# Attention kernel: the zeros in the unused corner of the weights go, and the row-sum matmul is split in two instead

## The reference

```python
scores = jnp.einsum('bhid,bhjd->bhij', Q, K) / jnp.sqrt(jnp.float32(hd))
delta = t[:, None] - t[None, :]
decay = jnp.where(delta < 0, 0.0, -delta.astype(jnp.float32) ** ALPHA)   # ALPHA = 1
scores = jnp.where(delta < 0, -jnp.inf, scores) + decay
attn = jax.nn.softmax(scores, axis=-1)
out = jnp.einsum('bhij,bhjd->bhid', attn, V)
```

## Time and profile before

| what | value |
|---|---|
| median of 3 runs | 1163.5 us (1161.0 to 1164.31) |
| the profiled execution's own time | 1161.0 us |
| its span, first to last instruction | 1159.4 us |
| around the span | 1.6 us |
| mean granted TensorE clock | 0.973 |
| PE busy | 1078.0 us, 93% of the span |
| DVE busy | 932.2 us, 80% |
| ACT busy | 796.4 us, 69% |
| POOL busy | 527.1 us, 45% |

### The profile page before, as it was taken

The page is one execution under the profiler, slowest core; times in us unless marked ns, Lnnn a source line. Parts: engine busy times, 40 slices in busy tenths (PEclk is TensorE's granted clock), DMA queues, the critical chain, the costliest instruction groups (busy, mean ns, idle before and its releaser), DMA issues.

```text
span 1159.4 us, 44674 instructions
## 1 busy us (share of the span) xinstructions
PE 1078.0 (93%) x18369; PEld 723.4 (62%) x18400; DVE 932.2 (80%) x2102; ACT 796.4 (69%) x1685; POOL 527.1 (45%) x969
## 2 busy tenths in 40 slices
PE   5899999999999999999999999999999999998551
PEld 3567666667666666676666666666666766664320
DVE  5858998888888888888988888888888888887563
ACT  5566777787766777777677777766777777666432
POOL 1133445454554544554545455545454555445331
PEclk9999999999999999999999999999999999999765
DMA  9666666766556667556676675655667656563231
GB/s 277 136 144 140 129 153 149 160 144 144 138 119 154 152 148 165 130 139 144 128 158 153 148 166 130 146 135 127 156 155 150 157 138 144 132 114 102 65 69 43
DMA packets 204833, 161.80 MB, mean 140 GB/s; under 512 B 150449, under 2 KB 150705, under 8 KB 204529
## 3 DMA queue, kind: packets, MB, share of 16 engines
q1 hardware_dynamic: 199888, 141.86, 55.6%
q0 software_dynamic: 4736, 17.04, 3.8%
HBM read 40.87 MB, written 16.78 MB: 50 GB/s over the span
## 4 chain that ended last, share of the span: by engine, by line
PE 80%; DVE 10%; issue 3%; SPq 3%; DMA 2%; ACT 2%; POOL 0%; DVEq 0%; POOLq 0%; ACTq 0%
PE f_job L1404 51%; PE f_st L1505 6%; PE f_o L1524 6%; PE f_o L1527 4%; PE f_job L1580 4%; PE f_job L1480 3%; PE f_job L1562 2%; SPq L357 2%; PE f_job L1570 1%; PE f_job L1488 1%; DMA f_x2Tl<-f_x2l 1%; DMA f_stacks<-f_mrow 1%; DVE f_rmax L1044 1%; DVE f_x L1117 1%; DVE f_x2l L1138 1%
## 5 line engine op out<-in xcount | busy, mean ns | idle before, releaser
L538 POOL TENSOR_SCALAR_AFFINE_SELECT f_PT<-f_PT 64x512 f32<-64x512 f32 (+1 forms) x256 | 181.9, 729 | 120.3 <-ACT f_PT L705 81.7
L1404 PE MATMUL f_job<-f_xTh,f_wqh 128*128 128x256 f16 x512 | 140.8, 275 | 15.2 <-DVE f_wkl L903 14.4
L1404 PE MATMUL f_job<-f_xTl,f_wqh 128*128 128x256 f16 x512 | 140.2, 274 | 0.0
L1404 PE MATMUL f_job<-f_xTh,f_wql 128*128 128x256 f16 x512 | 140.2, 274 | 0.0
L1404 PE MATMUL f_job<-f_xTh,f_wkh 128*128 128x256 f16 x512 | 140.0, 273 | 0.0
L1404 PE MATMUL f_job<-f_xTh,f_wkl 128*128 128x256 f16 x512 | 140.0, 273 | 0.0
L1404 PE MATMUL f_job<-f_xTl,f_wkh 128*128 128x256 f16 x512 | 139.9, 273 | 0.0
L675 ACT ACTIVATE f_stage<-f_job,f_bias 128x256 f16<-128x256 f32 x256 | 106.2, 466 | 34.1 <-PE f_job L1404 29.6
L1030 DVE SCALAR_TENSOR_TENSOR f_stage<-f_job,f_bias,f_stage 128x256 f16<-128x256 f32 x256 | 110.5, 477 | 20.5 <-ACT f_stage L675 18.4
L551 POOL TENSOR_TENSOR f_z<-f_z,f_x 128x512 f32<-128x512 f32 x62 | 78.1, 1280 | 101.7 <-ACT f_z L757 101.7
L705 ACT ACTIVATE f_PT<-f_st 128x512 f32<-128x512 f32 x192 | 113.0, 602 | 14.0 <-PE f_st L1505 14.0
(11 more groups left out here) (201 smaller groups left out, 3052.6 us busy)
## 6 DMA issues: line engine op xcount, KB each, us to landing
f_stacks<-f_stage SPq DMA_DIRECT2D x380, 128.0 KB
f_xin<-x SPq DMA_DIRECT2D x32, 512.0 KB, 4.1
f_x<-x SPq DMA_DIRECT2D x32, 512.0 KB, 4.4
out<-f_z POOLq DMA_DIRECT2D x31, 512.0 KB, 5.4
f_Vmix<-f_V SPq DMA_DIRECT2D x32, 256.0 KB, 3.3
f_Vmix<-f_V SPq DMA_DIRECT2D x64, 128.0 KB, 3.3
f_stacks<-rows_const SPq DMA_DIRECT2D x3, 512.0 KB, 4.7
f_stacks<-wqT SPq DMA_DIRECT2D x2, 512.0 KB, 5.1
```

The costliest lines, as they stand in the source:

```text
L538: nc.gpsimd.affine_select(out=d, in_=d, compare_op=ALU.is_ge, fill=0.0, base=odd * SUB, pattern=[[0, 4], [0, TP], [1, SUB]], channel_multi ...
L1404: mm = pe.matmul(dst, lhs[a](c), rhs[b](c), start=(n == 0), stop=(n == 3 * KC - 1))
```

## The change

DVE no longer zeroes the corner: clear_past, its 16 calls and its semaphore go, and with them weigh's wait. In exchange the row sums of an opening step no longer read the corner. There, the matmul of 256 columns for each of the four heads becomes two: one over the lower 64 partitions for the 64 columns of chunk 0, and one over 128 partitions for the other 192 columns. The four heads' matmuls of 64 columns come first, then the four of 192. In the other 24 steps of 32 the instructions of weigh are as before.

```diff
-            def clear_past(s, g):
-
-                until(dve, pv_done, 4 * s + g - 1)
-                nc.vector.memset(PT[g % 2][SUB:P, :, 0:SUB], 0.0).then_inc(past_cleared, 1)
-
...
             front_stats(2)
-            clear_past(0, 0)
-            clear_past(0, 1)
             for s in range(STEPS - 1):
...
                 if has(k):
                     normalise(k, 3)
-                if s and s % PER == 0:
-                    clear_past(s, 1)
                 if has(k - 1):
                     find_scale(k - 1, 0)
...
                 normalise(s, 2)
-                if n % PER == 0:
-                    clear_past(n, 0)
                 split_max(n)
...
                     pe.wait_ge(v_mixed, (s + 1) * (16 * 3))
-                if s % PER == 0 and g < 2:
-                    pe.wait_ge(past_cleared, 2 * (s // PER) + g + 1)
                 dst, weights = ps_o[g % 2], PT[g % 2]
...
-                for r in range(4):
-                    mm = pe.matmul(dst[r * HD:(r + 1) * HD, W2:D], ones[:], weights[:, r, :], start=True, stop=True)
+                for lo, hi in ((0, W2),) if s % PER else ((0, SUB), (SUB, W2)):
+                    keys, _ = values_of(s, lo // SUB)
+                    for r in range(4):
+                        mm = pe.matmul(dst[r * HD:(r + 1) * HD, W2 + lo:W2 + hi], ones[keys], weights[keys, r, lo:hi],
+                                       start=True, stop=True)
                 mm.then_inc(pv_done, 1)
```

More of the change, by code:

```diff
@@ L219, in fast_path @@
         masked = sem("masked")
-        past_cleared = sem("past_cleared")
         pv_done = sem("pv_done")
```

## The result

The changed kernel takes 1172.4 us (median of 4 runs, 1171.2 to 1173.2) where the kernel before takes 1163.0 (median of 4). The ratio is 1.0082, with a 95% interval of 1.0064 to 1.0099: slower by about 9 us. The profiled execution took 1170.79 us, its span 1168.7 us, 9.3 us longer than before's. Around the span it is 2.1 us where the kernel before has 1.6. Of the executions behind this document, one each of two kernels further down had a lower granted clock (0.56 and 0.84 against 0.97) and took 1837.8 and 1272.3 us; they are left out of all medians and ratios.

What follows compares the result with a forecast made beforehand. TensorE, a queue that never runs dry, was taken as the bound. Memsets -0.81, seven opening steps +7.56 and step 0 +0.81 gave +7.56 us: 1171.1 us on the median of 1163.5, 0.65% slower, range 1167 to 1174.

Steps and rivals of the forecast that it cites:

- The bound: Step loop: TensorE, busy 993.04 of 1000 us, never runs dry, so time added to it moves the end equally.
- The split's price: Row sums of each opening-step weigh: two more changes of tile shape, 64*32 and back to 128*32, cost 0.27 us.
- the upper bound of the range given: Price of the shape-change pair per opening weigh: at most 0.28 us, from the starts; the lower bound was 0.24.
- The rival of half the price: Row sums: loads of the long second part hide, one change paid, 0.135 us per weigh; +3.4 us, 1166.9 us, chance 8%.
- The rival that the split is free: Row sums of opening steps: splitting costs nothing, only the memsets' -0.81 us is left; 1162.7 us, chance 4%.
- What lies on the path: Opening weighs: all 28 of steps 4 to 28 count, 7.56 us, and three of step 0's four, 0.81 us.
- The memsets' part: VectorE's 16 memsets removed: only three lie on the path, -0.81 us together; the other 13 count as nothing.
- its first term: First two memsets, at 44.65 us ahead of the loop: TensorE's wait to 46.16 shortens, -0.54 us.
- The one at 313.08: TensorE's 0.32 us wait, reached from the memset at 305.90 through split_max, x2_low and a DMA; removal gives -0.27 us.
- the other memsets: The 13 memsets that end in no TensorE wait: hidden by TensorE's own work, counted as nothing.
- a sign that it was wrong: New waits appearing in the opening steps, listed among the observations that would show the forecast wrong.
- as a rival, for two other places: Later pv_done opens waits at the transposes or maxima's DMA, 0.3 us in 7 opening steps: +2.1, 1173.2 us, chance 12%.

Runs made afterwards that it cites:

- one pair more: Changed kernel with opening steps' row sums in four parts (chunk 0, chunk 1, chunk 0 again, chunks 2 and 3): 1184.1 us, ratio 1.0176.
- split in columns: Kernel before with opening steps' row sums split at column 64, both parts over 128 partitions, memsets kept: 1163.5 us, ratio 0.9990.
- full rows: Kernel before with chunk 0 of the opening steps over 128 partitions too, memsets kept: ratio 0.9957, median of six runs 1161.1 us.

## Why the prediction was right

**The bound** was read rightly: TensorE's queue doesn't run dry, and added time moves the end. An opening step grew by 1.22 us (step 16: 33.54 to 34.76) where four weighs account for 4 x 0.28 = 1.12; the other 0.1 is a new wait, described below, and the step ahead of it is 0.1 shorter.

**The split's price**, 0.27 us per weigh, taken from chunk 0 in a place between the same shapes, was 0.28: the upper bound of the range given. The rival of half the price falls: the long second group hides nothing. The rival that the split is free falls with it. That it is the change of shape, and not the 64 rows, the number of matmuls or the split, is shown by three runs: the same matmuls in another order, with one pair less (the cost is gone), the same split without a change of shape (no cost), and one pair more (0.28 us more, beside 0.11 for the columns). By the Trainium skill ("TensorEngine Tiling (Array Packing)", Key Properties), a change of tiling mode drains the engine; these runs agree as far as the price goes, and no row shows the drain itself. The page's other statement there, that different tiles run in parallel, agrees with the four heads' 8 matmuls of 64 columns in 0.11 us: on the whole array a float16 matmul of 512 columns takes 0.22 us to the next start (317.90 to 318.12), and eight of 64 columns one behind another would by that rate, an estimate, take 0.22.

**What lies on the path** of the loop was right: the loop's part of the span grew by 8.07 us, in the second profile by 7.3, where 28 x 0.28 is 7.84. Step 0 grew by 0.84 us, three weighs' worth as forecast.

**The memsets' part**, -0.81 us, was right in its first term and wrong in how it treated the loop. The first term is -0.54 us ahead of the loop: the idle time ahead of the norms' matmul shrank from 2.03 us to 1.30, by 0.73:

```profile
44.84 0.40 PE L1440 MATMUL f_job<-f_square,f_sel 128*32 128x512 bf16 x4 [1.30 <-DVE f_stage L1029]
...
95.77 0.17 PE L1466 MATMUL f_job<-f_stacks 107*32 107x24 f16 x1 [0.38 <-issue]
...
448.38 0.22 PE L1551 MATMUL f_job<-f_had,f_x2Th 128*128 128x128 f16 x1 [0.40 <-DMA f_x2Tl<-f_x2l]
449.56 0.63 PE L1493 MATMUL f_st<-f_stacks 128*64 128x128 f16 x16 [0.58 <-DMA f_stacks<-f_mrow]
...
584.06 0.38 PE L1392 MATMUL f_job<-f_woh,f_OTh 128*128 128x512 f16 x1 [0.16 <-POOL f_OTl L543]
```

This idle time is 2.03 to 2.12 us in all five profiles of kernels with the two memsets in that place, and 1.22 to 1.48 in the five without. How much of it lasts to the end is not settled, because other things between there and step 3 differ by more. The wait to 95.77 is not in the profile of the kernel before, nor in that with one pair more, and is in the other eight, 0.38 to 1.22 us, with and without memsets: it belongs to the execution. So do the waits for the transposes and for the maxima's DMA in the loop. The one at 313.08 that I credited with 0.27 us is gone, and two waits for a DMA stand at 448 and 449 us. A wait of 0.3 us for a DMA in one execution was no ground for a term of the sum.

The prediction then counted the other memsets as nothing, since no wait of TensorE named them. That step was wrong. The memset of buffer 0 stands ahead of split_max on VectorE, and turn_max on TensorE waits for split_max. In the kernel before, turn_max(16) starts 0.22 us behind the matmul ahead of it:

```profile
573.16 0.27 PE L1404 MATMUL f_job<-f_xTl,f_wkh 128*128 128x256 f16 x1
573.38 0.22 PE L1496 MATMUL f_job<-f_identh,f_mh 128*128 128x128 f16 x1
```

and in the changed kernel 0.11:

```profile
576.88 0.27 PE L1392 MATMUL f_job<-f_xTl,f_wkh 128*128 128x256 f16 x1
576.99 0.22 PE L1484 MATMUL f_job<-f_identh,f_mh 128*128 128x128 f16 x1
```

In the kernel before this distance is 0.21 to 0.22 us at each of the seven later opening steps and 0.11 at the other steps from 1 to 30; in the six kernels without the loop's memsets it is 0.11 at all of them. So seven memsets held TensorE up by 0.1 us each, 0.7 us in all. The matmul ahead is still running when turn_max starts, so the timeline marks no wait. The step ahead of an opening step takes 33.10 us with the memset (540.28 to 573.38) and 33.01 without (543.98 to 576.99).

These 0.7 us are given back. The last row of the first excerpt is a new wait, which stands in five of the seven later opening steps of the changed kernel; the prediction had named new waits in the opening steps as a sign that it was wrong, and priced them, as a rival, for two other places. The waits of TensorE, in total, times and longest, have it in the changed kernel as

```profile
PE f_job L1392 <- POOL f_OTl L543: 0.8, 5, 0.2
```

and the kernel that has lost only the loop's memsets as

```profile
PE f_job L1400 <- POOL f_OTl L544: 0.8, 5, 0.2
```

while the kernel with the split alone, all memsets kept, has one such wait:

```profile
PE f_job L1404 <- POOL f_OTl L544: 0.2, 1, 0.2
```

All six profiles of kernels without the loop's memsets show it, five times or six; the four with them (before, split alone, split in columns, full rows) show it once in all, at step 4 of the split alone, the one later opening step in these four where turn_max stands at 0.11 and not at 0.22. The opening step takes 33.54 us with the memset and 33.65 without (the kernel without the loop's memsets): TensorE comes earlier to out_product and waits there for GpSimd's low parts. What is gained ahead of the step is given back in it.

There is a second place where time goes, outside the first to last instruction. The device time less the span has a median of 1.6 us in the kernel before and in the three experiments that keep the loop's memsets, and of 2.0 to 2.9 us in all six that don't, up to 1.3 us more. With the loop's memsets alone taken out, the median of the span is 1161.1 us against 1162.3, and the device time is level with before (1164.1 and 1164.0). With the row sums in another order the span is 1161.2 us against 1162.6. So part of what leaving the memsets out takes off the span may be lost around it; in the first of the two kernels the difference in the span is within the noise. Why this time grows when memsets in the middle of the kernel go was not looked into, and stays open.

**The sum** was 7.6 us against 9.4 measured at first, and 8.2 with the interval's 6.2 to 10.1 in the second measurement. Of the 9.3 us of the profile's span, the parts can be read off: the split's 31 x 0.28 = 8.7 us (8.4 forecast); 0.9 less up to step 3, where 0.5 less was forecast and one execution differs from another by as much; 0.2 of other differences in the loop; and 1.26 us behind step 31, which were not forecast. That last stretch has the same instructions in all kernels. It takes 89.75 us before, 91.01 in the changed kernel, 90.14 and 92.47 in two kernels that have all memsets, so that its growth is the change's is not shown. The device time of this execution has 0.5 us more around the span on top. That the sum came out 1.8 us short at first and 0.6 in the second measurement is thus no measure of the small terms: the main term was right by its mechanism, and the others are of the size by which executions differ.

## What to carry to other kernels

When a matmul is cut so as to skip rows that hold zeros, look at what stands ahead of it and behind it. On a TensorE that hardly ever waits, half the rows saved nothing here, and a change from 128*32 to 64*32 and back cost 0.27 to 0.28 us, whether 64 or 192 columns followed. Put groups of one shape side by side, or give the odd one the shape of its neighbours and feed it zeros. Before work that is taken off an engine with slack gets a price, look for a wait that ends with it in more than one execution, and compare distances between starts too, since a delay of 0.1 us is marked nowhere; then ask what TensorE runs into when it comes earlier.

## What the runs showed that was not expected

The same kernel lost 1.7 us ahead of the loop in one execution and not in the other, with the granted clock. From 46 to 56 us the changed kernel's first profile has a mean clock of 1.00 (TensorE at its upper level, 2.4 GHz). The row gives the busy us of PE, PEld, DVE, ACT and POOL with their instructions, then the clock, the DMA share and GB/s:

```profile
46.00:56.00 10.00, 9.38 (x95) 6.43 (x92) 6.22 (x10) 6.01 (x16) 1.31 (x2) 1.00 0.31 71
```

and its second, of the same program, 0.83, so part of the stretch was at the lower level, 1.2 GHz:

```profile
46.00:56.00 10.00, 9.78 (x61) 6.10 (x58) 5.33 (x10) 4.27 (x11) 0.59 (x2) 0.83 0.08 23
```

TensorE had waited 1.30 us in the one and 1.48 us in the other for the norms' matmul, at 44.84 and 45.90 us. The work from turn_max's neighbour (45.63 and 46.68 us) to the first wait for ScalarE in step 0 (55.48 and 58.21) took 9.85 and 11.53 us. The same 0.83 stands in the profiles of the split alone, of full rows and of the kernel without the loop's memsets, and the other six have 1.00, the kernel before with its wait of 2.03 us among them, so neither the memsets nor the length of that wait tells the two apart. The 1.7 us are about a third of the spread between runs of one kernel (1161.2 to 1167.1 for the kernel before beside the first four), and larger than what the memsets could give.
